# Delta in a Mamba stack: one Softplus pass over four blocks at a time in place of Abs, Relu, Exp and Ln on ScalarE and a sum on GpSimd

## The chip, the cores and the metric

One core of one Trainium2 chip runs the whole program. The metric is the device time of one execution in microseconds (us). The engines are named as the profile names them: PE is TensorE (PEld its weight loads), DVE is VectorE, ACT is ScalarE, POOL is GpSimd, SP is SyncE.

## The reference, cut to what matters

Two Mamba layers over 8192 rows of 512 channels, with layer norms around them, and then a soft mixture of experts. The change is in the Mamba part, in the line that makes `delta`:

```python
xc, z = split(x @ W_in.T)                      # 1024 inner channels each
u = silu(conv4(xc) + b_c)
dt, Bm, Cm = split(u @ W_x.T)                  # 32, 16, 16
delta = softplus(dt @ W_dt.T + b_dt)           # the changed part
h_t = exp(delta_t * A) * h_{t-1} + (delta_t * u_t) * B_t    # 16 states for each channel
y_t = sum_n(h_t * C_t) + u_t * D
x = (y * silu(z)) @ W_out.T
```

Everything is fp32. The weights and inputs are random; softplus(x) was computed before as max(x, 0) + ln(1 + exp(-|x|)).

## The kernel before, in words

The 1024 inner channels are 8 blocks of 128 partitions. The 8192 rows are cut into 16 chunks of T = 512, which lie on the free axis. With two layers there are 32 chunk bodies, one after the other. A body has GROUPS = 32 groups (16 states for each of two halves of four blocks), and each group has four slots, one for each block: 128 slots, numbered s = 0 to 127 below. In slot s

- ACT writes one tile of `decay` = exp(delta * A) into a PSUM ring of four (`decay_of`, line 857; DEC_RING = 4),
- POOL writes, every second slot, one pair of tiles of `bu` = w * B, with w = delta * u (`inputs`, line 1086; p = s // 2 is the pair), into a ring of three pairs,
- DVE runs one scan h = decay * h + bu over 512 steps of time (`scan`, line 1166), and then `add_state` (line 1186), which multiplies a turned state tile with C and adds it to `acc`,
- PE turns the states of the group before (`turn_states`, line 589) into a PSUM ring of two tiles, `turn`. Two of eight such tiles are taken by ACT (`product`, line 873), the others by DVE. ACT also takes the `skip` tiles u * D (lines 597 and 880).

Around these fixed slots a timetable (`ORDER`, `timetable()`) spreads the projections of the next chunk: matmuls on PE into a second PSUM ring of two (`proj`), and on ACT what empties them. Every engine runs its instructions in the written order, and semaphores join them. The tile kinds `delta` (blocks 4 to 7 of this chunk) and `delta_next` (blocks 0 to 3 of the next) are emptied by ACT in `delta_parts`: w = |x| and delta = max(x, 0), one instruction each. When two blocks are there, `softplus_exp` (slot of the tile plus 1) and `softplus_ln` (plus 2) run over the pair (128 x 1024), and POOL adds (`sum_delta`) and multiplies with u (`product`), at the pairs p that `W_AT` lists. ACT takes delta tiles in slots 12, 18, 27, 32 and 84, 86, 93, 94. Exp and ln of the four pairs stand in slots 19 and 20, 33 and 34, 87 and 88, 95 and 96.

Silu of four blocks at once (`silu_u`, `silu_z`) is done in slots 43, 65, 116 and 129 (slot 1 of the next body). It is one ACTIVATE over 128 x 2048 between two table loads: one that the compiler puts ahead of it, and one asked for by `exp_tables()`, after which Exp and Ln can be used again.

Before the first body a prologue computes u, x_proj and delta for half of chunk 0, and only then can the first scan start.

Of the kernel before, what the change touches and what calls it, by code (L numbers as in the profile page):

```python
# [23 lines left out]
HB = NB // 2  # L24
# [33 lines left out]
W_AT = {13: ('sum', 2), 19: ('product', 2), 25: ('sum', 3), 27: ('product', 3), 47: ('sum_next', 0), 51:  # L58
        ('product_next', 0), 56: ('sum_next', 1), 63: ('product_next', 1)}
# [51 lines left out]
def timetable():  # L111
# [5 lines left out]
    for i, (kind, x, earliest) in enumerate(ORDER):  # L117
# [21 lines left out]
        if kind.startswith("delta") and x % 2 == 1:  # L139
            for q, part in enumerate(("exp", "ln")):  # L140
                take[late + 1 + q].append((part + kind[5:], x // 2, i))
# [147 lines left out]
def mamba_stack(nc, ctx, d, rstd, nmr):  # L289
# [75 lines left out]
    exp_set = sem("exp_set")  # L365
    softplus_set = sem("softplus_set")
    delta_set = sem("delta_set")
# [326 lines left out]
    def _(act):  # L694
# [83 lines left out]
        def delta_parts(src, X, b):  # L778

            if b % HB == 0:  # L780
                act.wait_ge(bu_set, X * PAIRS + (b // HB * (PAIRS // 2) - PAIRS // 2 + C_BU))
            act.activation(w[:, b, :], src, ACT.Abs)
            act.activation(delta[:, b, :], src, ACT.Relu).then_inc(proj_done, 1)

        def softplus_exp(X, freed, pair):
            act.wait_ge(proj_done, freed)
            act.activation(w[:, 2 * pair:2 * pair + 2, :], w[:, 2 * pair:2 * pair + 2, :], ACT.Exp, scale=-1.0).then_inc(exp_set, 1)

        def softplus_ln(X, pair):
            act.wait_ge(exp_set, X * HB + (pair + 1))  # L790
            act.activation(w[:, 2 * pair:2 * pair + 2, :], w[:, 2 * pair:2 * pair + 2, :], ACT.Ln, bias=1.0).then_inc(softplus_set, 1)  # L791
# [59 lines left out]
        def decay_of(G, kind, k, b):  # L851
# [3 lines left out]
            if n == 0:  # L855
                act.wait_ge(delta_set, G * HB + (blk // 2 + 1))
# [75 lines left out]
        for pair in range(HB // 2):  # L932
            softplus_exp(X, n + C_PROJ, pair)
            softplus_ln(X, pair)
# [3 lines left out]
        def take_tiles(G, position, kind, now, behind):  # L938


            for what, x, i in TAKE[position]:
# [4 lines left out]
                if not kind.has({"silu_u": "conv", "silu_z": "gate", "exp": "delta", "ln": "delta",  # L946
                                 "exp_next": "delta_next", "ln_next": "delta_next"}.get(what, what)):
                    continue
# [4 lines left out]
                if what not in ("silu_u", "silu_z", "exp", "ln", "exp_next", "ln_next"):  # L953
                    act.wait_ge(proj_full, full)
                if what == "delta":
                    delta_parts(src, G, x)
                if what == "exp":
                    softplus_exp(G, freed + 1, x)
                if what == "ln":
                    softplus_ln(G, x)  # L960
# [16 lines left out]
                if what == "exp_next":  # L977
                    softplus_exp(G + 1, freed + 1, x)
                if what == "ln_next":
                    softplus_ln(G + 1, x)  # L980
# [56 lines left out]
    def _(pool):  # L1037
# [26 lines left out]
        def sum_delta(X, pair):  # L1064

            lo = 2 * pair
            pool.wait_ge(softplus_set, X * HB + (pair + 1))
            pool.tensor_tensor(delta[:, lo:lo + 2, :], delta[:, lo:lo + 2, :], w[:, lo:lo + 2, :], ALU.add).then_inc(delta_set, 1)  # L1068

        def product(X, pair):  # L1070

            lo = 2 * pair
            pool.wait_ge(delta_set, X * HB + (pair + 1))
            pool.wait_ge(u_set, X * 2 + (pair * 2 // HB + 1))
# [37 lines left out]
        for pair in range(HB // 2):  # L1112
            sum_delta(0, pair)
            product(0, pair)

        def delta_w(G, what, pair):
            X = G + what.endswith("_next")
            if what.startswith("sum"):
                sum_delta(X, pair)
            else:  # L1120
                product(X, pair)

        def body(G, kind):
            for p in range(PAIRS):
                what, pair = W_AT.get(p, ("", 0))
                if what and kind.has(what.replace("sum", "delta").replace("product", "delta")):
# [864 lines left out]
```

## Time and profile before

| | |
|---|---|
| median of 3 runs | 7865.79 us (7862.75 to 7871.68) |
| the profiled execution, its own time | 7866.45 us |
| its span in the trace | 7864.7 us |
| first scan of the first body | 124.83 us |
| length of one body, layer 0, layer 1 | about 221.75 us, about 221.0 us |

The span is what the trace covers; the profiled execution took 1.75 us more than that and 0.7 us more than the median of the runs. All times in the timeline rows are us from the start of the span. In a timeline row the first number is the start, the second how long it took (from the start of the first to the end of the last where several are merged, xN), and in brackets stands how long the engine had been idle and what released it.

### The profile page before, as it was taken

The page shows a single profiled execution, that of the slowest core. Times are in us where ns is not written, and L with a number is a line of the kernel's source. Part 1 is how long each engine was busy: PE and PEld are TensorE (multiplying, and loading weights), DVE is VectorE, ACT ScalarE, POOL GpSimd, SP SyncE. Part 2 cuts the span into 40 slices and gives each one's busy share as a digit, 9 for nine tenths or more (in the row PEclk, how much of TensorE's full clock was granted, in tenths as well). Part 3 has the DMA queues.
Part 4 walks back from the last instruction along what each step waited for, and adds up shares of the span by engine and source line. Part 5 has one row for each costly group of instructions (what it writes and reads, how often), then busy time and mean ns, then how long its engine had stood idle before and what let it go on. Part 6 is the DMA issues. An engine that isn't in the chain of part 4 may idle for free. (4 is left out here: it accounts for less than half of the span.)

```text
span 7864.7 us, 100984 instructions
## 1 busy us (share of the span) xinstructions
PE 7131.2 (91%) x31188; PEld 4059.3 (52%) x31188; DVE 7350.3 (93%) x8247; ACT 5888.5 (75%) x11211; POOL 6606.0 (84%) x2870
## 2 busy tenths in 40 slices
PE   7899999999999999998999999999999999977899
PEld 3455555555555555554555555555555555544765
DVE  3999999999999999999999999999999999997745
ACT  6787888887877887777777777777777777764653
POOL 3999999999999999999999999999999999996020
PEclk9999999999999999999999999999999999988798
DMA  2122111112211221121211111111111111111754
GB/s 85 61 65 66 60 65 58 55 61 65 66 65 61 65 65 56 55 66 66 66 56 49 56 52 49 53 54 56 54 56 49 56 54 47 53 49 62 261 208 150
DMA packets 230983, 549.65 MB, mean 70 GB/s; under 512 B 27120, under 2 KB 27376, under 8 KB 210864
## 3 DMA queue, kind: packets, MB, share of 16 engines
q1 hardware_dynamic: 201776, 491.81, 19.5%
q10 hardware_dynamic: 28672, 51.39, 1.7%
q8 instruction: 252, 4.13, 0.2%
q14 instruction: 283, 2.32, 0.1%
HBM read 441.39 MB, written 101.71 MB: 69 GB/s over the span
## 5 line engine op out<-in xcount | busy, mean ns | idle before, releaser
L1086 POOL TENSOR_TENSOR bu<-w,b_rep 128x1024 f32<-128x1024 f32 x2048 | 4810.1, 2368 | 538.9 <-DVE h L1166 529.4
L1166 DVE TENSOR_TENSOR_SCAN h<-decay,h_last,bu 128x512 f32<-128x512 f32 x3840 | 4797.7, 1269 | 13.9 <-ACT decay L857 13.9
L589 PEld LDWEIGHTS turn<-ident_m,h 128*128 128x128 f32 x16384 | 1952.3, 142 | 2702.8 <-DVE acc L1186 1314.3
L857 ACT ACTIVATE decay<-delta,neg_a 128x512 f32<-128x512 f32 x4096 | 2777.0, 690 | 647.6 <-DVE h L1166 611.6
L589 PE MATMUL turn<-ident_m,h 128*128 128x128 f32 x16384 | 2558.4, 280 | 421.0 <-DVE acc L1186 348.0
L1186 DVE SCALAR_TENSOR_TENSOR acc<-turn,c_now,acc 128x512 f32<-128x512 f32 x3072 | 2227.2, 725 | 72.2 <-ACT c_now L885 43.1
L873 ACT ACTIVATE prod<-turn,c_now 128x512 f32<-128x512 f32 x1024 | 701.0, 685 | 504.5 <-PE turn L589 368.6
L1101 POOL TENSOR_TENSOR prod<-prod 128x1024 f32<-128x1024 f32 x448 | 1058.7, 2363 | 10.6 <-ACT prod L873 10.6
L511 PE MATMUL proj<-x_conv,w_in 128*128 128x512 f32 x2048 | 1046.8, 603 | 4.2 <-ACT x_conv L847 0.9
L511 PE MATMUL proj<-conv_in,conv_diag 128*128 128x512 f32 x2048 | 1024.8, 594 | 0.2 <-ACT halo L750 0.2
L511 PE MATMUL proj<-x_gate,w_in 128*128 128x512 f32 x2048 | 1019.8, 595 | 0.0
L511 PE MATMUL proj<-zy,w_out 128*128 128x512 f32 x1024 | 505.6, 596 | 23.0 <-ACT u L758 20.5
L511 PE MATMUL proj<-w_out,zy 128*128 128x512 f32 x1024 | 504.4, 599 | 0.9 <-DVE zy L1195 0.9
L1166 DVE TENSOR_TENSOR_SCAN h<-decay,zeros_m,bu 128x512 f32<-128x512 f32 x256 | 319.3, 1268 | 128.0 <-POOL bu L1086 124.8
L511 PEld LDWEIGHTS proj<-x_conv,w_in 128*128 128x128 f32 x2048 | 328.2, 193 | 123.3 <-issue 91.7
L511 PEld LDWEIGHTS proj<-conv_in,conv_diag 128*128 128x128 f32 x2048 | 325.8, 191 | 106.7 <-issue 103.6
L511 PEld LDWEIGHTS proj<-x_gate,w_in 128*128 128x128 f32 x2048 | 324.1, 191 | 98.0 <-issue 91.8
L1068 POOL TENSOR_TENSOR delta<-delta,w 128x1024 f32<-128x1024 f32 x128 | 302.4, 2362 | 48.0 <-ACT w L791 48.0
L597 PE MATMUL turn<-d_diag,u 128*128 128x128 f32 x2048 | 288.6, 285 | 48.5 <-DVE acc L1186 44.2
L740 ACT ACTIVATE conv_diag<-ident_m,par 128x128 f32<-128x128 f32 x1024 | 326.2, 394 | 0.8 <-ACT x_conv L847 0.5
L1075 POOL TENSOR_TENSOR w<-delta,u 128x1024 f32<-128x1024 f32 x128 | 302.9, 2366 | 0.3
L597 PEld LDWEIGHTS turn<-d_diag,u 128*128 128x128 f32 x2048 | 252.8, 194 | 74.3 <-DVE acc L1186 60.1
(157 smaller groups left out, 5777.7 us busy)
## 6 DMA issues: line engine op xcount, KB each, us to landing
b_rep<-b_rows SPq DMA_DIRECT2D x1024, 256.0 KB, 3.2
x_gate<-xt SPq DMA_DIRECT2D x32, 1024.0 KB, 6.9
xt<-stage ACTq DMA_DIRECT2D x128, 256.0 KB, 2.4
x_conv<-xt SPq DMA_DIRECT2D x31, 1024.0 KB, 6.9
x_gate<-in_x_dram SPq DMA_DIRECT2D x16, 1024.0 KB, 6.6
x_l<-in_x_dram SPq DMA_DIRECT2D x16, 1024.0 KB, 8.7
m_l<-xt SPq DMA_DIRECT2D x16, 1024.0 KB, 4.9
x<-x_l SPq DMA_DIRECT2D x16, 1024.0 KB, 4.9
```

The source lines that it names most:

```text
L511: mm = pe.matmul(out[0:lhs.shape[1], :], lhs, rhs, start=n == 0, stop=n == count - 1)
L589: mm = pe.transpose(out[:, b * P:(b + 1) * P], h[:, (G * GROUPS + k) % H_RING, b, j * P:(j + 1) * P], ident[:])
L597: mm = pe.matmul(out[:, b * P:(b + 1) * P], u[:, hf * HB + b, j * P:(j + 1) * P], d_diag[:, hf * HB + b, :], start=True, stop=True)
L740: act.activation(conv_diag[:, b % 2, k, :], ident[:], ACT.Copy, scale=par[:, STATES + k, b:b + 1])
L857: act.activation(decay[:, (G * SLOTS_BODY + s) % DEC_RING, :], delta[:, blk, :], ACT.Exp, scale=neg_a[:, n, blk:blk + 1]).then_inc(decay_s ...
L873: act.activation(prod[:, V_BUFFER[q], k % 2, :], turn[:, BANK[tile], :], ACT.Copy, scale=c_now[:, j, n:n + 1]).then_inc(v_done, 1)
L1068: pool.tensor_tensor(delta[:, lo:lo + 2, :], delta[:, lo:lo + 2, :], w[:, lo:lo + 2, :], ALU.add).then_inc(delta_set, 1)
L1075: pool.tensor_tensor(w[:, lo:lo + 2, :], delta[:, lo:lo + 2, :], u[:, lo:lo + 2, :], ALU.mult).then_inc(w_set, 2)
L1086: pool.tensor_tensor(bu[:, (G * PAIRS + s // 2) % BU_RING, :, :], w[:, blk:blk + 2, :], b_rep[:, g % B_RING, :].unsqueeze(1).to_broadcast( ...
L1101: pool.tensor_tensor(total, total, prod[:, V_BUFFER[q]], ALU.add).then_inc(vsum_set, 1)
L1166: dve.tensor_tensor_scan(h[:, (G * GROUPS + k) % H_RING, b, :], decay[:, (G * SLOTS_BODY + s) % DEC_RING, :], bu[:, (G * PAIRS + s // 2) % ...
L1186: dve.scalar_tensor_tensor(out, src, scalar, out, ALU.mult, ALU.add).then_inc(x_done, 1)
```

## The change

ACT copies a projected delta tile from PSUM to `delta` with one COPY, instead of writing |x| and max(x, 0). When all four blocks of a half are there, one ACTIVATE Softplus over 128 x 2048 works in place on `delta`, in the slot in which exp of the second pair stood, followed by `exp_tables()`. The passes exp and ln, POOL's sum, and two semaphores go. `decay_of` waits once for each half instead of once for each block. POOL's four products with u are moved by `W_AT`: from p = 19, 27, 51, 63 to 25, 28, 58, 61.

```diff
@@ -55,8 +55,7 @@
 V_SUM_AT = (11, 10, 11, 11, 11, 11, 11, 9, 9, 9, 11, 11, 11, 10, 11, 9)
 JOIN_AT = (41, 72)
 
-W_AT = {13: ('sum', 2), 19: ('product', 2), 25: ('sum', 3), 27: ('product', 3), 47: ('sum_next', 0), 51:
-        ('product_next', 0), 56: ('sum_next', 1), 63: ('product_next', 1)}
+W_AT = {25: ('product', 2), 28: ('product', 3), 58: ('product_next', 0), 61: ('product_next', 1)}
 
 
 NORM_SLOTS = (10, 11, 13, 14, 20, 22, 25, 27, 28, 30, 31, 51, 52, 53, 56)
@@ -136,9 +135,8 @@
         if kind == "conv_half":
             take[late - TAPS_LEAD].append(("taps", x, i))
         take[late].append((kind, x, i))
-        if kind.startswith("delta") and x % 2 == 1:
-            for q, part in enumerate(("exp", "ln")):
-                take[late + 1 + q].append((part + kind[5:], x // 2, i))
+        if kind.startswith("delta") and x % HB == HB - 1:
+            take[late + 1].append(("softplus" + kind[5:], x // HB, i))
         if kind == "conv" and x % HB == HB - 1:
             take[late + SILU_LATER[x // HB]].append(("silu_u", x // HB, i))
         if kind == "gate" and x % HB == HB - 1:
@@ -779,16 +775,12 @@
 
             if b % HB == 0:
                 act.wait_ge(bu_set, X * PAIRS + (b // HB * (PAIRS // 2) - PAIRS // 2 + C_BU))
-            act.activation(w[:, b, :], src, ACT.Abs)
-            act.activation(delta[:, b, :], src, ACT.Relu).then_inc(proj_done, 1)
-
-        def softplus_exp(X, freed, pair):
+            act.copy(delta[:, b, :], src).then_inc(proj_done, 1)
+
+        def softplus(freed, hf):
             act.wait_ge(proj_done, freed)
-            act.activation(w[:, 2 * pair:2 * pair + 2, :], w[:, 2 * pair:2 * pair + 2, :], ACT.Exp, scale=-1.0).then_inc(exp_set, 1)
-
-        def softplus_ln(X, pair):
-            act.wait_ge(exp_set, X * HB + (pair + 1))
-            act.activation(w[:, 2 * pair:2 * pair + 2, :], w[:, 2 * pair:2 * pair + 2, :], ACT.Ln, bias=1.0).then_inc(softplus_set, 1)
+            act.activation(delta[:, hf * HB:hf * HB + HB, :], delta[:, hf * HB:hf * HB + HB, :], ACT.Softplus).then_inc(softplus_set, 2)
+            exp_tables()
 
         def gate(src, b):
 
@@ -852,8 +844,8 @@
             hf, n = divmod(k, STATES)
             blk, s = hf * HB + b, HB * k + b
             act.wait_ge(scanned, G * SLOTS_BODY + (s + 1 - DEC_RING + C_SCAN))
-            if n == 0:
-                act.wait_ge(delta_set, G * HB + (blk // 2 + 1))
+            if n == 0 and b == 0:
+                act.wait_ge(softplus_set, G * HB + (hf * 2 + 2))
             act.activation(decay[:, (G * SLOTS_BODY + s) % DEC_RING, :], delta[:, blk, :], ACT.Exp,
                            scale=neg_a[:, n, blk:blk + 1]).then_inc(decay_set, 1)
 
@@ -1061,17 +1045,13 @@
         bias(0)
         bias(1)
 
-        def sum_delta(X, pair):
+        def product(X, pair):
 
             lo = 2 * pair
-            pool.wait_ge(softplus_set, X * HB + (pair + 1))
-            pool.tensor_tensor(delta[:, lo:lo + 2, :], delta[:, lo:lo + 2, :], w[:, lo:lo + 2, :], ALU.add).then_inc(delta_set, 1)
-
-        def product(X, pair):
-
-            lo = 2 * pair
-            pool.wait_ge(delta_set, X * HB + (pair + 1))
-            pool.wait_ge(u_set, X * 2 + (pair * 2 // HB + 1))
+            half = lo // HB
+            pool.wait_ge(softplus_set, X * HB + (half * 2 + 2))
+            pool.wait_ge(u_set, X * 2 + (half + 1))
+            pool.wait_ge(bu_set, X * PAIRS + (half * (PAIRS // 2) - PAIRS // 2 + C_BU))
             pool.tensor_tensor(w[:, lo:lo + 2, :], delta[:, lo:lo + 2, :], u[:, lo:lo + 2, :], ALU.mult).then_inc(w_set, 2)
 
         def inputs(G, k, pr):
```

What this does to the order of the instructions is shown at three places of a steady body of layer 0. The first is ACT around slot 33, before the change. `acc<-turn` is the copy of a skip tile (slot 33), `w<-w` is exp and then ln over a pair, and `conv_diag` (slot 35) belongs to the convolution.

```order
L782 ACTIVATE w<-proj 128x512
L783 ACTIVATE delta<-proj 128x512
L857 ACTIVATE decay<-delta,neg_a 128x512
L880 COPY acc<-turn 128x512
L787 ACTIVATE w<-w 128x1024
L857 ACTIVATE decay<-delta,neg_a 128x512
L791 ACTIVATE w<-w 128x1024
L857 ACTIVATE decay<-delta,neg_a 128x512
L880 COPY acc<-turn 128x512
L740 ACTIVATE conv_diag<-ident_m,par 128x128 x4
```

And the same place in the changed kernel, with that file's own line numbers:

```order
L778 COPY delta<-proj 128x512
L849 ACTIVATE decay<-delta,neg_a 128x512
L872 COPY acc<-turn 128x512
L782 ACT_TABLE_LOAD
L782 ACTIVATE delta<-delta 128x2048
L701 ACT_TABLE_LOAD
L849 ACTIVATE decay<-delta,neg_a 128x512 x2
L872 COPY acc<-turn 128x512
L736 ACTIVATE conv_diag<-ident_m,par 128x128 x4
```

Between the decay tiles of slots 33 and 34 a load, a pass over four blocks and another load now stand, where one pass over two blocks stood; nothing stands between those of 34 and 35.

The second place is ACT around slot 95, before the change. `prod<-turn` is a state tile that ACT takes for the sum over the states (slots 94 and 95).

```order
L857 ACTIVATE decay<-delta,neg_a 128x512
L873 ACTIVATE prod<-turn,c_now 128x512
L782 ACTIVATE w<-proj 128x512
L783 ACTIVATE delta<-proj 128x512
L857 ACTIVATE decay<-delta,neg_a 128x512
L873 ACTIVATE prod<-turn,c_now 128x512
L787 ACTIVATE w<-w 128x1024
L857 ACTIVATE decay<-delta,neg_a 128x512
L890 COPY h_last<-h 128x4
L791 ACTIVATE w<-w 128x1024
```

And in the changed kernel:

```order
L849 ACTIVATE decay<-delta,neg_a 128x512
L865 ACTIVATE prod<-turn,c_now 128x512
L778 COPY delta<-proj 128x512
L849 ACTIVATE decay<-delta,neg_a 128x512
L865 ACTIVATE prod<-turn,c_now 128x512
L782 ACT_TABLE_LOAD
L782 ACTIVATE delta<-delta 128x2048
L701 ACT_TABLE_LOAD
L849 ACTIVATE decay<-delta,neg_a 128x512
L882 COPY h_last<-h 128x4
```

Here too the whole group now stands between two decay tiles, those of slots 95 and 96.

The third place is POOL from p = 23 to p = 31 of the same body, before the change (`delta<-delta,w` is the sum, `w<-delta,u` the product, `prod<-prod` a sum over states).

```order
L1101 TENSOR_TENSOR prod<-prod 128x1024
L1086 TENSOR_TENSOR bu<-w,b_rep 128x1024
L1068 TENSOR_TENSOR delta<-delta,w 128x1024
L1086 TENSOR_TENSOR bu<-w,b_rep 128x1024 x2
L1075 TENSOR_TENSOR w<-delta,u 128x1024
L1086 TENSOR_TENSOR bu<-w,b_rep 128x1024
L1101 TENSOR_TENSOR prod<-prod 128x1024
L1086 TENSOR_TENSOR bu<-w,b_rep 128x1024 x4
```

And in the changed kernel:

```order
L1081 TENSOR_TENSOR prod<-prod 128x1024
L1066 TENSOR_TENSOR bu<-w,b_rep 128x1024
L1055 TENSOR_TENSOR w<-delta,u 128x1024
L1066 TENSOR_TENSOR bu<-w,b_rep 128x1024 x3
L1081 TENSOR_TENSOR prod<-prod 128x1024
L1055 TENSOR_TENSOR w<-delta,u 128x1024
L1066 TENSOR_TENSOR bu<-w,b_rep 128x1024 x4
```

The product of blocks 4 and 5 stands where the sum of blocks 6 and 7 stood, that of blocks 6 and 7 one pair later than before, and the number of long instructions in the stretch is the same.

## Rows read from the trace of the kernel before

**Rows 1.** The page's first part: busy time, share of the span, instructions.

```profile
PE 7131.2 (91%) x31188; PEld 4059.3 (52%) x31188; DVE 7350.3 (93%) x8247; ACT 5888.5 (75%) x11211; POOL 6606.0 (84%) x2870
```

**Rows 2.** Busy time in one body: stretch, length, PE, PEld, DVE, ACT, POOL.

```profile
3002.40:3224.10 221.70, 205.33 (x917) 115.83 (x916) 218.89 (x233) 178.81 (x345) 205.04 (x90) 0.99 0.18 59
```

**Rows 3.** Waits in the whole span: us in total, times, longest.

```profile
DVE h L1166 <- POOL bu L1086: 124.8, 1, 124.8
...
DVE acc L1186 <- ACT c_now L885: 43.1, 31, 1.4
...
DVE h L1166 <- ACT decay L857: 17.1, 33, 1.9
...
POOL bu L1086 <- DVE h L1166: 529.4, 568, 2.7
```

**Rows 4.** Groups by line: count, busy us, mean ns of one, idle before.

```profile
L1068 POOL TENSOR_TENSOR delta<-delta,w 128x1024 f32<-128x1024 f32 x128 | 302.4, 2362 | 48.0 <-ACT w L791 48.0
...
L796 ACT COPY zy<-proj 128x512 f32<-128x512 f32 x256 | 149.3, 583 | 83.7 <-PE proj L511 83.3
```

**Rows 5.** Timeline of ACT at slot 43, a Silu between its two loads.

```profile
3075.03 1.28 ACT L762 ACT_TABLE_LOAD   x1
3076.33 1.91 ACT L762 ACTIVATE u<-u 128x2048 f32<-128x2048 f32 x1
3078.26 1.28 ACT L705 ACT_TABLE_LOAD   x1
3079.55 1.28 ACT L740 ACTIVATE conv_diag<-ident_m,par 128x128 f32<-128x128 f32 x4
```

**Rows 6.** Timeline of all engines, slots 31 to 35.

```profile
3058.50 1.16 PE L597 MATMUL turn<-d_diag,u 128*128 128x128 f32 x8 [0.34 <-DVE acc L1186]
...
3059.70 0.59 ACT L880 COPY acc<-turn 128x512 f32<-128x512 f32 x1 [0.88 <-PE turn L597]
...
3060.18 1.06 ACT L787 ACTIVATE w<-w 128x1024 f32<-128x1024 f32 x1
...
3061.14 0.68 ACT L857 ACTIVATE decay<-delta,neg_a 128x512 f32<-128x512 f32 x1
...
3063.86 1.27 DVE L1166 TENSOR_TENSOR_SCAN h<-decay,h_last,bu 128x512 f32<-128x512 f32 x1
...
3064.08 0.59 ACT L880 COPY acc<-turn 128x512 f32<-128x512 f32 x1 [0.70 <-PE turn L597]
```

**Rows 7.** Timeline of all engines, slots 37 to 40.

```profile
3070.11 0.68 ACT L873 ACTIVATE prod<-turn,c_now 128x512 f32<-128x512 f32 x1
...
3070.84 1.16 PE L597 MATMUL turn<-d_diag,u 128*128 128x128 f32 x8
...
3074.06 0.60 PE L589 MATMUL turn<-ident_m,h 128*128 128x128 f32 x4
...
3074.74 0.72 DVE L1186 SCALAR_TENSOR_TENSOR acc<-turn,c_now,acc 128x512 f32<-128x512 f32 x1
```

**Rows 8.** Timeline of all engines, slots 93 to 96.

```profile
3162.82 0.60 PE L589 MATMUL turn<-ident_m,h 128*128 128x128 f32 x4
...
3163.45 0.70 ACT L873 ACTIVATE prod<-turn,c_now 128x512 f32<-128x512 f32 x1
...
3164.99 0.69 ACT L857 ACTIVATE decay<-delta,neg_a 128x512 f32<-128x512 f32 x1
...
3168.32 1.27 DVE L1166 TENSOR_TENSOR_SCAN h<-decay,h_last,bu 128x512 f32<-128x512 f32 x1
```

**Rows 9.** Timeline of ACT and POOL around p = 25, slot 48.

```profile
3083.69 2.37 POOL L1068 TENSOR_TENSOR delta<-delta,w 128x1024 f32<-128x1024 f32 x1
...
3085.89 0.69 ACT L758 ACTIVATE u<-proj,par 128x512 f32<-128x512 f32 x1
```

**Rows 10.** Timeline of ACT and POOL at the end of the prologue.

```profile
109.85 0.59 ACT L783 ACTIVATE delta<-proj 128x512 f32<-128x512 f32 x1
...
112.69 2.35 POOL L1068 TENSOR_TENSOR delta<-delta,w 128x1024 f32<-128x1024 f32 x1 [48.03 <-ACT w L791]
...
122.27 4.65 POOL L1086 TENSOR_TENSOR bu<-w,b_rep 128x1024 f32<-128x1024 f32 x2
```

More of the change, by code:

```diff
@@ L364, in mamba_stack @@
     z_set = sem("z_set")
-    exp_set = sem("exp_set")
     softplus_set = sem("softplus_set")
-    delta_set = sem("delta_set")
     w_set = sem("w_set")
@@ L931, in _ @@
             n += 1
-        for pair in range(HB // 2):
-            softplus_exp(X, n + C_PROJ, pair)
-            softplus_ln(X, pair)
+        softplus(n + C_PROJ, 0)
         set_a(0, 0)
@@ L945, in take_tiles @@
                     continue
-                if not kind.has({"silu_u": "conv", "silu_z": "gate", "exp": "delta", "ln": "delta",
-                                 "exp_next": "delta_next", "ln_next": "delta_next"}.get(what, what)):
+                if not kind.has({"silu_u": "conv", "silu_z": "gate", "softplus": "delta",
+                                 "softplus_next": "delta_next"}.get(what, what)):
                     continue
@@ L952, in take_tiles @@
                 src = proj[:, kind.place[i] % RING, :]
-                if what not in ("silu_u", "silu_z", "exp", "ln", "exp_next", "ln_next"):
+                if what not in ("silu_u", "silu_z", "softplus", "softplus_next"):
                     act.wait_ge(proj_full, full)
@@ L956, in take_tiles @@
                     delta_parts(src, G, x)
[L957 to L960, printed above, removed]
+                if what in ("softplus", "softplus_next"):
+                    softplus(freed + 1, x)
                 if what == "conv_half":
@@ L976, in take_tiles @@
                     delta_parts(src, G + 1, x)
[L977 to L980, printed above, removed]
                 if what == "gate":
@@ L1112, in _ @@
         for pair in range(HB // 2):
-            sum_delta(0, pair)
             product(0, pair)
         def delta_w(G, what, pair):
[L1117 to L1121, printed above, removed]
+            product(G + what.endswith("_next"), pair)
         def body(G, kind):
@@ L1125, in body @@
                 what, pair = W_AT.get(p, ("", 0))
-                if what and kind.has(what.replace("sum", "delta").replace("product", "delta")):
+                if what and kind.has(what.replace("product", "delta")):
                     delta_w(G, what, pair)
```

## The prediction

> **What bounds the kernel now.** I began with the page's first part: DVE is busy for 93% of the span, PE for 91%, POOL for 84%, ACT for 75% [rows 1]. Shares say little here, so I took one body by itself. Of its 221.70 us DVE works 218.89 and is idle for 2.8; PE works 205, POOL 205 and ACT 179 [rows 2]. The Mamba part, 32 such bodies, is bound by DVE, whose work the change doesn't touch. Work taken from ACT or POOL can shorten a body by those 2.8 us at most; work put on them can lengthen it wherever DVE comes to wait. In the table of waits, DVE waited for POOL once, before the first scan (124.8 us), never in a body; 31 times for `c_now` (43.1 us); and 33 times for a decay tile (17.1 us), about once a body [rows 3]. POOL waited 568 times for scans (529.4 us), so it runs as far ahead as its ring lets it. So the question is when ACT delivers each decay tile, and I read that in the timeline, having counted the scans of the body that begins at 3002.36 to know the slots.
>
> **What is removed.** In a body of 221 us ACT loses 8 Abs and 8 Relu, whose place 8 copies of 583 ns take [rows 4], and four passes each of exp and ln; POOL loses four sums of 2.36 us [rows 4]. In a body that is worth nothing by itself: DVE waits for neither there, except for the decay tile at slot 44 and for `c_now` at slot 8, and neither place is near the removed passes (slots 19, 20, 33, 34, 87, 88, 95, 96).
>
> **What a Softplus costs on ACT.** The trace has no Softplus. The nearest row is Silu of the same shape between the same two loads: load 1.28 us, pass 1.91 us, load 1.28 us, and from the first load's start at 3075.03 to the next instruction at 3079.55 it is 4.52 us, in which no decay tile is made [rows 5]. From below, the pass can't take less than exp over half the elements, 1.06 us [rows 6], and above I allow a doubled pass, 3.8 us. I take 1.91, the value of the row with the same form. Before, one exp stood in that place and held the next decay tile back by 0.85 us (from the end of the copy, 3059.70 + 0.59 = 3060.29, to 3061.14) [rows 6]. The decay tile behind each Softplus therefore comes 4.52 + 0.01 - 0.85 = 3.68 us later, unless ACT can start the group earlier.
>
> **Slot 33.** ACT can't start earlier here: the copy in front of the group began at 3059.70 after 0.88 us of waiting for PE's skip tile, and PE had itself waited for DVE to free a bank [rows 6]. What the cheaper delta copies save just lengthens this wait. The decay tile of slot 34 was ready at 3061.14 + 0.68 = 3061.82 and its scan began at 3063.86: 2.04 us to spare. DVE will wait 3.68 - 2.04 = 1.65 us. A part of the lateness goes on through the turn ring. ACT takes the skip tile of slot 33 after two decay tiles of 0.61 us each: the first now starts at 3060.29 + 4.53 = 3064.82, so the copy at 3066.04, against 3064.08 before [rows 6], 1.96 us late, 0.3 more than DVE. From there ACT works without a pause to the product at 3070.11, whose end at 3070.79 frees the bank that PE takes at 3070.84 for the last skip tile; and at slot 40 DVE takes its tile at 3074.74, only 0.08 us after PE has made it (3074.06 + 0.60) [rows 7]. So 0.3 less 0.08, about 0.2 us more, reach DVE. Slot 33 costs 1.85 us in each of 32 bodies: 59.2 us. In the bodies where ACT and PE have other margins (the first and last) it can be a little more.
>
> **Slot 95.** The product in front of the group follows PE's tile (3162.82 + 0.60 = 3163.42, taken at 3163.45) [rows 8], so the copies saved before it don't help here either. The decay tile of slot 96 was ready at 3164.99 + 0.69 = 3165.68, its scan began at 3168.32, 2.64 us to spare. DVE waits 3.68 - 2.64 = 1.04 us. Behind it ACT has no ln to do any more and DVE's next tiles are ready on PE, so I count nothing for later. The last body has no `delta_next`: 31 x 1.04 = 32.2 us.
>
> **POOL.** It does two long instructions fewer in each half of a body, and what hides the rest is its ring of three pairs [rows 3]. From p = 23 to 28, where it has least to spare, the number of long instructions stays the same. One edge is new: the copy of u at slot 48 waits for the product of blocks 4 and 5, which overwrites nothing before it is done. That product now stands where the sum started at 3083.69, and so ends at 3086.06; the copy began at 3085.89 [rows 9]. That is 0.2 us on ACT at most, less what ACT is already late by; I take nothing. If that cover were gone, it would be 0.2 x 32 = 6 us.
>
> **Prologue.** The first scan waits for four POOL instructions, from 112.69 to the first `bu` at 122.27 [rows 10], 9.58 us; two of them, 4.63 us, stay. The last delta tile was done at 109.85 + 0.59 = 110.44; with one copy for each tile I put it at 109.55 (between 0 and 2 us earlier). Load and pass take 3.2 us from there, POOL starts at 112.85 and `bu` at 117.5: 4.8 us gained.
>
> **Sum.** 59.2 + 32.2 - 4.8 = 86.6 us. On the profiled execution's own 7866.45 us that is 7953; the median of the runs is 0.7 us less, which I leave out.
>
> **A rule that speaks against this.** The trace has the load at 1.28 us and the pass 0.02 us behind it [rows 5], with no pause in between. The Trainium skill, "ScalarE: Activation LUTs", section "What ACT_TABLE_LOAD costs", gives about 2.66 us for every switch, the load and a drain of 1.38 us; by that the group would take 7.2 us, and the total would be about 8125. The rows don't show that drain between load and pass, so they decide.
>
> **The rivals.**
>
> (a) The group hides: ACT is further ahead than I read, and DVE sees only the prologue, 7862, no change. For it: four Silu groups a body cost DVE only 17.1 us in all [rows 3]. Against it: Silu at slot 43 already makes DVE wait, and the spare times of 2.04 and 2.64 are both below 3.68 [rows 6, 8]. 5%.
>
> (b) On the other side: the relief of ACT reaches the wait for `c_now`. It is worth 43.1 us, with the prologue 48, so 7818. It decides if ACT is late at slot 8 because of its own load over the whole body; but the last of the removed passes stands at slot 96, 40 slots before, and behind it ACT waits for PE and DVE again and again. Even then slots 33 and 95 would have to cost under 32 us together to be faster by the bound. 3%.
>
> (c) Softplus is slower than Silu. With a doubled pass both waits grow by 1.91 us: 63 x 1.91 = 120, so 8074. No row speaks for it: exp, 1.06 us for 1024 elements [rows 6], and Silu, 1.91 us for 2048 [rows 5], lie on one line of 0.83 ns for each. 4%.
>
> (d) A switch to Softplus's set costs more than one to Silu's, as a pause beside each load. With a pause as long as the load itself, 1.28 us [rows 5], it would be 63 x 2.56 = 161, so 8114. The rows 3076.33 and 3079.55 follow their loads by 0.02 and 0.01 us [rows 5]. 2%. This is the case to which the drain of the page would come.
>
> (e) The waits are right, but part comes back: a later DVE gives PE and ACT time, and the decay wait at slot 44 (17.1 us in all, [rows 3]) goes, or the group at 95 starts 0.5 us earlier (15 us). Then about 7925. 13%.
>
> **How the numbers follow.** The forecast (two new waits a body, 1.6 to 2.2 us and 0.9 to 1.3 us, which is 7931 to 7972) has 73%. The range takes in (e) below and, above, 0.4 us more a body for what goes on through the turn ring: 7924 to 7985. A measurement of this kernel can't tell less than 0.2%, 16 us, from no change. Faster 0.03 (b), same 0.06 (a), slower 0.91.
>
> **What would show it.** In the new trace: 64 Softplus rows of 1.91 us, 128 more loads; in DVE's table of waits a decay wait of 1.6 to 1.7 us at slot 34 and one of about 1.0 us at slot 96, some 95 in number and 100 us in total, against 33 and 17.1; bodies of about 224.7 and 223.9 us; the first scan at about 120. The `c_now` wait stays at 43 us. I am wrong if the scan at slot 34 starts without a wait, if Softplus takes another time than Silu, or if the waits for PE's turn tiles grow by more than 0.3 us a body.

## The result and the profile after

The changed kernel takes 7956.87 us in the median of 4 runs (7954.51 to 7967.72), the kernel before beside it 7866.81 us: 1.0117 times as long, 95% interval 1.0099 to 1.0134. The profiled execution took 7956.39 us, its span 7954.6 us, 89.9 us more than before. The page's first part, against [rows 1]:

```profile
PE 7155.0 (90%) x31188; PEld 4052.4 (51%) x31188; DVE 7359.8 (93%) x8247; ACT 5846.8 (74%) x10891; POOL 6321.3 (79%) x2742
```

POOL works 285 us less and ACT 42 us less, and the kernel is 90 us longer. The body of the same number as in [rows 2], in the same columns:

```profile
3042.91:3267.68 224.77, 205.23 (x916) 114.51 (x916) 219.19 (x234) 177.53 (x335) 196.19 (x86) 1.00 0.18 57
```

DVE works as long as before, within 0.3 us, and is idle for 5.6 us in place of 2.8. The waits, against [rows 3]:

```profile
POOL bu L1066 <- DVE h L1141: 918.1, 949, 3.8
...
DVE h L1141 <- POOL bu L1066: 121.5, 1, 121.5
DVE h L1141 <- ACT decay L849: 103.6, 96, 2.4
DVE norm_sq_l L1380 <- PE ssq_l L1487: 73.3, 16, 10.6
...
DVE acc L1161 <- ACT c_now L877: 43.1, 31, 1.4
```

DVE now waits for a decay tile 96 times in place of 33, 103.6 us in place of 17.1; the wait for `c_now` is the same 43.1 us. POOL's freed time went into its own waiting for DVE, 918 us in place of 529. The groups by line, against [rows 4]:

```profile
L782 ACT ACTIVATE delta<-delta 128x2048 f32<-128x2048 f32 x64 | 122.3, 1911 | 0.7
...
L782 ACT ACT_TABLE_LOAD x64 | 82.1, 1283 | 1.2
```

Where the time stands, by the start of each scan in both traces: the first scan is 3.3 us earlier (121.51 against 124.83), the 32 bodies are 100.4 us longer, and what follows the last scan is 7.1 us shorter. The first body is 7.16 us longer, each of the next 30 between 3.00 and 3.10 us, the last 1.34 us. In a body in the middle, the extra time to the next scan is 1.67 us at slot 33, 0.20 at slot 40, 0.09 at slot 43 and 1.09 at slot 95; all other slots are within 0.05 us. The timeline at slots 31 to 35, against [rows 6]:

```profile
3099.01 1.16 PE L593 MATMUL turn<-d_diag,u 128*128 128x128 f32 x8 [0.33 <-DVE acc L1161]
...
3100.20 0.58 ACT L872 COPY acc<-turn 128x512 f32<-128x512 f32 x1 [1.37 <-PE turn L593]
3100.81 1.28 ACT L782 ACT_TABLE_LOAD   x1
3102.10 1.91 ACT L782 ACTIVATE delta<-delta 128x2048 f32<-128x2048 f32 x1
3104.03 1.28 ACT L701 ACT_TABLE_LOAD   x1
3105.32 1.30 ACT L849 ACTIVATE decay<-delta,neg_a 128x512 f32<-128x512 f32 x2
...
3106.05 1.28 DVE L1141 TENSOR_TENSOR_SCAN h<-decay,h_last,bu 128x512 f32<-128x512 f32 x1 [1.60 <-ACT decay L849]
```

ACT had waited 1.37 us for PE's skip tile, so the group could not start sooner; it runs from 3100.81 to 3105.32, and the scan behind it waits. (The row counts 1.60 us of idle time; from scan to scan it is 1.67.) At slot 40, against [rows 7]:

```profile
3114.52 0.58 ACT L872 COPY acc<-turn 128x512 f32<-128x512 f32 x1 [0.55 <-PE turn L593]
...
3116.47 0.60 PE L585 MATMUL turn<-ident_m,h 128*128 128x128 f32 x4
...
3117.11 0.75 DVE L1161 SCALAR_TENSOR_TENSOR acc<-turn,c_now,acc 128x512 f32<-128x512 f32 x1
```

DVE takes this tile 0.04 us after PE has made it: the bank came late. At slots 95 and 96, against [rows 8]:

```profile
3205.26 0.60 PE L585 MATMUL turn<-ident_m,h 128*128 128x128 f32 x4
...
3205.89 0.69 ACT L865 ACTIVATE prod<-turn,c_now 128x512 f32<-128x512 f32 x1 [0.40 <-PE turn L585]
3206.60 1.28 ACT L782 ACT_TABLE_LOAD   x1
...
3211.12 0.69 ACT L849 ACTIVATE decay<-delta,neg_a 128x512 f32<-128x512 f32 x1
...
3211.84 1.28 DVE L1141 TENSOR_TENSOR_SCAN h<-decay,h_last,bu 128x512 f32<-128x512 f32 x1 [1.00 <-ACT decay L849]
```

The end of the prologue, against [rows 10]:

```profile
105.33 0.58 ACT L764 COPY xdbl<-proj 64x512 f32<-64x512 f32 x1 [7.94 <-PE proj L507]
...
110.34 0.59 ACT L778 COPY delta<-proj 128x512 f32<-128x512 f32 x1 [0.27 <-PE proj L560]
...
114.34 4.64 POOL L1055 TENSOR_TENSOR w<-delta,u 128x1024 f32<-128x1024 f32 x2 [47.67 <-ACT delta L782]
118.94 6.96 POOL L1066 TENSOR_TENSOR bu<-w,b_rep 128x1024 f32<-128x1024 f32 x3
```

### The profile page after: what moved, and what is told of

Its sections match the earlier page's. It is cut to its first block and busy times, and to the rows that moved or that the text cites. A ratio compares the mean times of both kernels' runs of the same rounds, so it can differ in the third digit from the quotient of the medians.

```text
span 7954.6 us, 100536 instructions
## 1 busy us (share of the span) xinstructions
PE 7155.0 (90%) x31188; PEld 4052.4 (51%) x31188; DVE 7359.8 (93%) x8247; ACT 5846.8 (74%) x10891; POOL 6321.3 (79%) x2742
## 5 line engine op out<-in xcount | busy, mean ns | idle before, releaser
L1161 DVE SCALAR_TENSOR_TENSOR acc<-turn,c_now,acc 128x512 f32<-128x512 f32 x3072 | 2229.0, 726 | 76.8 <-ACT c_now L877 43.1
L601 PE MATMUL turn<-ident_m,acc 128*128 128x128 f32 x1024 | 166.4, 286 | 126.6 <-DVE acc L1161 114.4
```

Source lines behind the costliest of these rows:

```text
L601: mm = pe.transpose(out[:, j * P:(j + 1) * P], acc[:, hf, j, b * P:(b + 1) * P], ident[:])
L1161: dve.scalar_tensor_tensor(out, src, scalar, out, ALU.mult, ALU.add).then_inc(x_done, 1)
```

## The experiments

The theory: a group on ACT costs DVE its own length, less the pass that it replaced, less the time that the decay tile behind it had to spare; nothing else of the change costs. The rivals: the loads cost by their number; GpSimd's new places cost; the stall is not of ACT's length. In each run the medians of the kernel before were between 7864.7 and 7866.5 us. Lengths of bodies and slots are taken from the starts of the scans and given as the difference from before. In the diffs `...` stands for what is left out.

**No switch, and no long group.** Exp takes Softplus's place, with the table that is there, so that delta has other values.

```diff
-            act.activation(..., ACT.Softplus).then_inc(softplus_set, 2)
-            exp_tables()
+            act.activation(..., ACT.Exp).then_inc(softplus_set, 2)
```

> The changed kernel with Exp in place of Softplus, so that delta is exp(x) and its values differ, and without the two table loads around it: the same pass over 128 x 2048 in the same two slots. My theory is that a group on ACT costs DVE the time by which it makes the next decay tile later, less what that tile had to spare before. The pass alone holds the next tile back by 1.82 us, 0.97 more than exp of a pair did, under the 2.04 and 2.64 us to spare at slots 34 and 96: no new wait, bodies of 221.75 and 221.0 us as before, and a prologue about 6 us shorter: about 7861. If the pass over four blocks at once makes DVE wait and not the loads, it stays above 7900; if each load is paid for in full wherever it stands, it would be 7957 - 164 = 7793.

Measured 7863.3 us, ratio 0.9992 (0.9983 to 1.0002). Waits of DVE:

```profile
DVE h L1140 <- ACT decay L848: 17.0, 33, 1.9
```

The decay waits are those of before. With the two loads gone and all else kept (the copies, the pass over four blocks, POOL's places, one wait for each half), nothing is left of the 90 us. Nor is there a gain beyond the noise from all the work that the change removes.

**The group of the next blocks three slots later.**

```diff
-            take[late + 1].append(("softplus" + kind[5:], x // HB, i))
+            take[late + (4 if kind == "delta_next" else 1)].append(("softplus" + kind[5:], x // HB, i))
```

> The changed kernel with the Softplus of blocks 0 to 3 in slot 98 in place of slot 95. The tile behind it, of slot 99, had 5.3 us to spare before and 3.6 after the change, with the lateness from slot 95 in it; the group makes it 4.5 us later. My theory: the wait of 1.09 us at slot 96 goes and no other comes, 7957 - 35 = 7922, with bodies of 223.7 and 223.0 us. The rival, that a load costs its time wherever it stands, has 7957; one that the turn or projection ring passes the lateness on from slots 98 to 104 has 7930 to 7960.

Measured 7929.08 us, ratio 1.0076 (1.0061 to 1.0091). Waits of DVE:

```profile
DVE h L1141 <- ACT decay L849: 72.1, 65, 2.5
```

The 1.09 us at slot 95 is gone and nothing came in its place: bodies in the middle are 1.97 us longer, 1.68 of it at slot 33, 0.20 at slot 40 and 0.09 at slot 43. So the place sets the cost. The time is 7 us over the expectation. The bodies are as expected; in the profiled runs the stage after them is 8.5 us longer than in the changed kernel (more on it below).

**Both groups moved.** The time tiles 6 and 7 are made earlier, so that the group of blocks 4 to 7 stands in slot 28.

```diff
-         5, 0), ('conv', 1, 0), ('conv_half', 3, 0), ('delta', 6, 0), ('conv', 2, 0), ('delta', 7, 0), ('conv_half',
+         5, 0), ('conv', 1, 0), ('delta', 6, 0), ('conv_half', 3, 0), ('delta', 7, 0), ('conv', 2, 0), ('conv_half',
...
-            take[late + 1].append(("softplus" + kind[5:], x // HB, i))
+            take[late + (4 if kind == "delta_next" else 0)].append(("softplus" + kind[5:], x // HB, i))
```

> As the run before, and the delta projections of blocks 6 and 7 earlier in the order on PE, so that ACT has the last in slot 28 and does the other Softplus in the same slot, with the tile of slot 29 having 5.5 us to spare. My theory: the waits at slots 34, 40 and the growth at 44 go as well (1.97 us in each body), bodies of 221.8 and 221.0 us, and only the prologue's gain is left: 7860, up to 7875 if the moved matmuls press on PE. The rival that loads cost their time anywhere has 7957.

Measured 7880.84 us, ratio 1.0021 (1.0012 to 1.0030). What the changed kernel lost at slots 33, 40, 43 and 95 is gone, but each body in the middle is still 0.5 us longer, nearly all of it at slot 29, and the time is 6 us over the upper end of what I expected. Its timeline there:

```profile
3059.31 1.28 ACT L701 ACT_TABLE_LOAD   x1
...
3060.47 0.60 PE L585 MATMUL turn<-ident_m,h 128*128 128x128 f32 x4
...
3061.85 0.67 ACT L865 ACTIVATE prod<-turn,c_now 128x512 f32<-128x512 f32 x1
...
3062.57 0.65 PE L601 MATMUL turn<-ident_m,acc 128*128 128x128 f32 x4 [0.20 <-ACT prod L865]
...
3063.26 0.69 DVE L1170 TENSOR_TENSOR zy<-turn,zy 128x512 f32<-128x512 f32 x1 [0.28 <-PE turn L601]
```

The decay tiles have the time to spare now, but ACT takes PE's tile (ended 3061.07) only at 3061.85; that holds a bank, PE makes the y tile late, and DVE waits for it. ACT has two dates to keep, and I had reckoned only with one.

**Softplus by pairs.** Four groups a body in place of two, each over 128 x 1024, so twice the loads.

```diff
-        if kind.startswith("delta") and x % HB == HB - 1:
-            take[late + 1].append(("softplus" + kind[5:], x // HB, i))
+        if kind.startswith("delta") and x % 2 == 1:
+            take[late + 1].append(("softplus" + kind[5:], x // 2, i))
...
+            act.activation(delta[:, 2 * pair:2 * pair + 2, :], delta[:, 2 * pair:2 * pair + 2, :], ACT.Softplus).then_inc(softplus_set, 1)
```

> The changed kernel with Softplus over pairs of blocks (128 x 1024), each between two loads, in the four slots in which exp stood (19, 33, 87, 95): twice the groups and loads. A group takes 1.28 + 1.06 + 1.28 + 0.04 = 3.67 us and makes the next tile 2.83 us later than exp did. With 2.98, 2.04, 2.37 to 2.64 and 2.64 us to spare, less what the cheaper copies give, my theory has waits of 0, 0.8 (0.2 more through the turn ring), 0 to 0.4 and 0.2 us: 1.2 to 1.6 us in a body, 7900 to 7918, so faster than the changed kernel in spite of twice the loads. If the cost is that of the loads, it doubles: about 8045.

Measured 7927.84 us, ratio 1.0077 (1.0062 to 1.0093). Waits of DVE:

```profile
DVE h L1142 <- ACT decay L849: 52.8, 99, 1.9
```

Twice the loads and 29 us less than the change. Slot 33 costs 0.82 us in place of 1.67, slot 95 0.23 in place of 1.09: both less by what the group is shorter, a pass over 1024 elements less. New are 0.23 us at slot 87 and, in layer 0, 0.41 at slot 22, where DVE waits for PE's y tile as in the run before this one. That makes 1.60 us a body in layer 1, as forecast, but 2.02 in layer 0 and 7.8 in the first body, and the time was some 10 us above the range that I gave.

**GpSimd's places alone, in the kernel before.**

```diff
-W_AT = {13: ('sum', 2), 19: ('product', 2), 25: ('sum', 3), 27: ('product', 3), 47: ('sum_next', 0), 51:
-        ('product_next', 0), 56: ('sum_next', 1), 63: ('product_next', 1)}
+W_AT = {13: ('sum', 2), 25: ('product', 2), 19: ('sum', 3), 28: ('product', 3), 47: ('sum_next', 0), 58:
+        ('product_next', 0), 51: ('sum_next', 1), 61: ('product_next', 1)}
```

> The kernel before, with GpSimd's products of w and sums of delta put where the changed kernel has its products (pairs 25, 28, 58 and 61 for the products); nothing else. My theory, that the time comes from ScalarE's group alone and GpSimd's places are worth nothing: 7866, within 10 of it, and each body within 0.2 us of before. The rival, that the later products hold up the copy of u or the product of the next pair: some 0.2 us a body, 7872; if the places were the cause of most of the change's loss, 7900 or more.

Measured 7871.87 us, ratio 1.0007 (0.9997 to 1.0016). Bodies of layer 0 are some 0.2 us longer (at slot 62; the first two are 2.2 and 1.9 longer), those of layer 1 are as before. The 5 us by which the medians differ are within what this measurement can't tell from no change. So the places are no cause of the 90 us; in the changed kernel slot 62 isn't longer at all. But the rival's 0.2 us a body is there in layer 0, and the rows tell how it comes about. In the sixth body ACT's product in slot 61 waits 1.15 us for POOL's sum over states, in place of 0.69 before, and so frees its bank later; in slot 62 DVE waits 0.72 us for PE's tile, in place of 0.49.

**The group at slot 26.** From here on the versions go after what was left of the two moved groups. Here both time tiles are made ahead of the half product 3 and taken in slots 23 and 24.

```diff
-         5, 0), ('conv', 1, 0), ('conv_half', 3, 0), ('delta', 6, 0), ('conv', 2, 0), ('delta', 7, 0), ('conv_half',
+         5, 0), ('conv', 1, 0), ('delta', 6, 0), ('delta', 7, 0), ('conv_half', 3, 0), ('conv', 2, 0), ('conv_half',
...
-            take[late + 1].append(("softplus" + kind[5:], x // HB, i))
+            take[late + (4 if kind == "delta_next" else 2)].append(("softplus" + kind[5:], x // HB, i))
```

> The changed kernel with both groups where ScalarE has the time for them: the time tiles 6 and 7 are made before the half product 3 (taken in slots 23 and 24), Softplus of blocks 4 to 7 stands in slot 26, that of the next blocks in slot 98. My theory, that only the places of the two groups cost: the body loses the 0.5 us at slot 29 that the version with the group in slot 28 had, since ScalarE starts the group two slots earlier and is level again when its product of slot 30 is due; bodies within 0.2 us of before, and the whole 7860 to 7872. The rival, that a group of 4.47 us fits nowhere at that stage, since about 4.6 to 5 us is the most by which ScalarE is ahead: again 0.3 to 0.8 us a body, 7876 to 7892.

Measured 7868.52 us, ratio 1.0003 (0.9994 to 1.0012): not to be told from before. But only the bodies of layer 1 are as before (within 0.01 us, but for three), with the last two of layer 0; the first is 4.3 us longer and the 13 behind it 0.43, all at slot 29. So theory and rival each hold in one layer.

**SiLU one slot later too**, added to the version in slot 26, to use the decay wait that is there in every body of the kernel before, and **SiLU one slot later in the kernel before**:

```diff
-SILU_LATER = (1, 2, 4, 3)
+SILU_LATER = (2, 2, 4, 3)
```

> The version before this one, with SiLU of u's first half in slot 44 in place of 43, where the kernel before already waits 0.56 us for a decay in every body. By my theory of spare time the decay of slot 44 is then in time and those of 45 and 46 come 0.05 and 0.25 us late: 0.3 us a body won, 10 us in all, 7850 to 7862, faster than the kernel before. The rival, that ScalarE's two products of slots 46 and 47 then come late and the turn ring holds PE: no gain or a loss, 7865 to 7885.

> The kernel before with only SiLU of u's first half in slot 44 in place of 43, beside the last one, to tell what this move gives without the change. By my theory the same 0.3 us a body, 7852 to 7860. The rival, the turn ring: 7866 or more.

Measured 7880.42 us, ratio 1.0017 (1.0008 to 1.0026), and 7862.18 us, ratio 0.9995 (0.9986 to 1.0004). In both, slot 43 is 0.56 us shorter, and slots 44, 45 and 46 are 0.09, 0.21 and 0.17 us longer: 0.09 us a body won where I had expected 0.3. The wait was moved, not removed; the one at slot 46 I hadn't foreseen. Both times are over the ranges that I gave, the first by 18 us and inside the rival's.

In the first of them, nine bodies are a further 1 to 1.7 us longer, six at slot 24 and three at slots 62 to 64, and DVE waits there for a tile of PE. The trace shows TensorE slower just there, and at neither place in any other body but the last. In the body that begins at 4565.92 its granted clock, as a share of the full 2.4 GHz, is 0.92 in slot 22, 0.50 (the lower of its two levels, 1.2 GHz) in slot 23 and 0.80 in slot 24; in the body before that, with slot 24 as usual, it is 1.00 in all of them. In both bodies PE had worked for just 0.73 of the 2.41 us of slot 22, so what made the clock fall in one and not in the other stays open. Single bodies of the other versions that are 1 us longer at slot 24, and the second body of the run with GpSimd's places, at slots 63 and 64, show slow matmuls of the same kind.

**The group at slot 25**, to the version in slot 26.

```diff
-            take[late + (4 if kind == "delta_next" else 2)].append(("softplus" + kind[5:], x // HB, i))
+            take[late + (4 if kind == "delta_next" else 1)].append(("softplus" + kind[5:], x // HB, i))
```

> As the version with the group in slot 26, but in slot 25, and the loads and Softplus of the next blocks in slot 98 again. The profile of the version in slot 26 has its layer 1 bodies at 0.00 us over before and its layer 0 bodies at 0.43, all in slot 29, where ScalarE takes the product of slot 28 1.15 us after PE ended it. In slot 25 the group is one slot more ahead of that product. My theory, that only the place costs: layer 0 bodies within 0.1 us of before too, 14 bodies of 0.43 less, 6 us: 7858 to 7868, no difference from before that this can tell. The rival, that the decay of slot 26 is late, since ScalarE is only 4.83 us ahead there in layer 0: again 0.3 to 0.5 us a body, and as before 7864 to 7874.

Measured 7876.02 us, ratio 1.0015 (1.0006 to 1.0024), though its profiled run took 7867.11. Bodies of layer 1 are as before, those of layer 0 still 0.46 us longer at slot 29. The rival's 0.3 to 0.5 us a body came out, but not its mechanism, since the decay of slot 26 is in time. The timeline of a body of layer 0:

```profile
3056.66 0.71 ACT L817 ACTIVATE stage<-x_gate,neg_mean 128x512 f32<-128x512 f32 x1
...
3058.06 0.72 ACT L817 ACTIVATE stage<-x_gate,neg_mean 128x512 f32<-128x512 f32 x1
...
3058.93 0.66 PE L585 MATMUL turn<-ident_m,h 128*128 128x128 f32 x4 [0.32 <-DVE acc L1161]
...
3060.77 0.67 ACT L865 ACTIVATE prod<-turn,c_now 128x512 f32<-128x512 f32 x1
...
3062.19 0.69 DVE L1170 TENSOR_TENSOR zy<-turn,zy 128x512 f32<-128x512 f32 x1 [0.36 <-PE turn L601]
```

ACT takes the tile 1.2 us after PE ended it at 3059.59. In front of it stand two squares of a normalisation, which only the first 14 bodies do.

**The normalisation's steps later.** To the version before this:

```diff
-NORM_SLOTS = (10, 11, 13, 14, 20, 22, 25, 27, 28, 30, 31, 51, 52, 53, 56)
+NORM_SLOTS = (10, 11, 13, 14, 20, 22, 31, 33, 34, 36, 37, 51, 52, 53, 56)
```

> The version with the groups in slots 25 and 98, and of the normalisation of a later block, which only layer 0 bodies do, three squares and the two small steps after them taken out of slots 25, 27, 28, 30 and 31 and put into 31, 33, 34, 36 and 37. The trace of the version before this one shows two of these squares, some 0.9 us each, between the end of ScalarE's group and the product of slot 28, taken 1.19 us after PE ended it. My theory, that ScalarE's lateness at slot 28 is all that is left: the layer 0 bodies, at 0.46 us over before, come to within 0.1 us of it, 14 of them, 6 us: 5 to 7 us under the version before. The rival, that the squares are late in their new places and hold the products of slots 31 to 38: again 0.3 to 1 us a body, no better than the version before.

Measured 7868.03 us, ratio 1.0001 (0.9992 to 1.0010). ACT now waits for PE there:

```profile
3056.05 0.69 ACT L865 ACTIVATE prod<-turn,c_now 128x512 f32<-128x512 f32 x1 [0.93 <-PE turn L585]
```

The 0.46 us at slot 29 is gone, so it was ACT's lateness at this tile. But 0.20 us at slot 40 and 0.09 at slot 43 are back, as in the changed kernel: the squares, now at 31 to 34, make ACT late for the skip tiles, and a body of layer 0 is 0.28 us longer. So part of the lateness was only moved: I had expected these bodies within 0.1 us of before, and the rival had 0.3 or more. The time is 8 us under the version in slot 25, but the bodies together are only 3 us shorter. Its last two bodies, without the squares, are 1.1 us longer at slot 24, with the slow matmuls told of above. Layer 1 stays as before.

**A second load of the same table, and one of another.** The first adds `exp_tables()` a second time, the second:

```diff
             act.activation(..., ACT.Softplus).then_inc(softplus_set, 2)
+            act.preload_act_table_set("silu_and_others")
             exp_tables()
```

> The changed kernel with the table load that follows Softplus issued twice, so each group of 4.47 us becomes 5.75. My theory, that a group costs its own length less the time that ScalarE is ahead, and the two places of the changed kernel are already past that: each of the 1.28 us is paid in full, 2.56 us a body, 79 us over 31 bodies: 8036, and 8030 to 8042. If the second load of a set that is there costs nothing, 7957. The rival, that the stalls of the changed kernel are of another cause than ScalarE's length (a wait for POOL or for PE's turn ring): a small part of it, under 8000. If each load also stops ScalarE's queue for longer than its row, over 8050.

> The changed kernel with one table load more in each group, of SiLU's table, between Softplus and the load of Exp's, so that a group is 5.75 us and not 4.47. (In the run with the second load of the same table the trace showed no more loads than before: 193 and 64, so nothing was tried there.) My theory, that both places are past the time by which ScalarE is ahead: the 1.28 us is paid in full twice a body, 2.56 us, 79 us over 31 bodies, 8036, and 8030 to 8045 with growth at the turn ring. The rival, that the stalls of the changed kernel are not of ScalarE's length: under 8000. If each load also stops ScalarE's queue for longer than its row, over 8050.

The first had no load more than the changed kernel:

```profile
L701 ACT ACT_TABLE_LOAD x193 | 247.6, 1283 | 7.5 <-POOL ident_m L1037 4.1
```

So the 8036 us that I expected of a longer group wasn't tested by it, and it is a second measurement of the same instructions: 7966.05 us, ratio 1.0129 (1.0115 to 1.0144), bodies together 101.0 us longer against the 100.4 of the changed kernel. The second measured 8075.2 us, ratio 1.0265 (1.0249 to 1.0281). Its timeline at slots 33 to 38, and its decay waits:

```profile
3150.15 1.91 ACT L782 ACTIVATE delta<-delta 128x2048 f32<-128x2048 f32 x1
3152.08 1.28 ACT L783 ACT_TABLE_LOAD   x1
3153.37 1.28 ACT L701 ACT_TABLE_LOAD   x1
3154.66 1.30 ACT L850 ACTIVATE decay<-delta,neg_a 128x512 f32<-128x512 f32 x2
...
3155.39 1.28 DVE L1142 TENSOR_TENSOR_SCAN h<-decay,h_last,bu 128x512 f32<-128x512 f32 x1 [2.89 <-ACT decay L850]
3155.91 0.57 ACT L873 COPY acc<-turn 128x512 f32<-128x512 f32 x1
...
3156.53 1.07 PE L585 MATMUL turn<-ident_m,h 128*128 128x128 f32 x4 [2.46 <-ACT acc L873]
...
3157.39 2.06 PE L593 MATMUL turn<-d_diag,u 128*128 128x128 f32 x8
...
3159.49 0.59 ACT L873 COPY acc<-turn 128x512 f32<-128x512 f32 x1 [0.54 <-PE turn L593]
...
3163.10 0.60 PE L585 MATMUL turn<-ident_m,h 128*128 128x128 f32 x4
...
3163.74 0.75 DVE L1162 SCALAR_TENSOR_TENSOR acc<-turn,c_now,acc 128x512 f32<-128x512 f32 x1 [0.99 <-PE turn L585]
```

```profile
DVE h L1142 <- ACT decay L850: 181.1, 96, 3.8
```

Slot 33 is 2.96 us longer than before in place of 1.67, slot 95 2.37 in place of 1.09: both by 1.29 us more, the length of the row of a load, as expected. The time is still 39 us over the expectation. Of the 115.8 us by which its bodies together are longer than those of the changed kernel, 82.0 stand at these two slots, 33.8 at slot 38 (and 9.9 less at slots 40 and 43) and 8.2 at slot 102. Slot 38 is 0.85 to 1.56 us longer in 26 of the first 31 bodies, 1.12 in the body of [rows 2]; in the other five, all of layer 1, it is as before, and slots 40 and 43 have the 0.20 and 0.09 us of the changed kernel.

The rows tell how slot 38 comes to it. The skip tile of slot 33, which PE ended at 3152.60, is taken at 3155.91, and PE has waited 2.46 us for that. Then it runs at half its pace: the eight matmuls of the next skip tile take 2.06 us, where those of the one before took 1.06. So that tile is only there at 3159.45, and the tile for slot 38 at 3163.70, after DVE has waited 0.99 us for it. TensorE's granted clock is 1.00 up to 3153.89, 0.59 from 3156.49 to 3157.29, 0.50 to 3159.19, 0.67 to 3160.49 and 1.00 again behind that. In the body that begins at 4006.73, one of the five, PE waits the same 2.46 us, the clock stays at 1.00 through these slots, and slot 38 is as before. All of the 26 bodies have such slow matmuls at slots 35 to 37, and none of the five has. In the changed kernel PE waits 1.17 us at this place and the clock stays at 1.00. So the growth that I had put at nothing is TensorE's slower clock behind the pause, and not lateness that grows by itself in the turn ring; what lets the clock stay up in the five bodies is open. That the time is over 8050 is not the rival of a longer stop of ACT's queue: the two slots behind the loads show 1.29 us more, which is the row's length, and no more.

## Why the prediction was right, step by step

**The bound.** DVE bound the bodies before and does after; taking 285 us of work from POOL and 42 us from ACT gave DVE nothing. The run with Exp shows this with all of the removals in place: 7863.3 us.

**The group on ACT.** 4.52 us was taken from SiLU's rows; it is 4.51 (3100.81 to 3105.32), with the pass at 1911 ns. Rivals (c) and (d) fall with that row: no doubled pass, no pause beside the loads. Of the Trainium skill, "ScalarE: Activation LUTs", section "What ACT_TABLE_LOAD costs": its drain of 1.38 us for each switch is not seen here either, since one switch more made DVE 1.29 us later.

**Slot 33.** 1.65 us was forecast and 1.67 measured; 0.2 through the turn ring was forecast, and 0.20 at slot 40 and 0.09 at slot 43 measured. The second of these was missed. (3.68 less 2.04 is 1.64; that changes nothing.)

**Slot 95.** 1.04 forecast, 1.09 measured, and nothing behind it, as said. Moving that group alone took exactly this away.

**POOL.** Nothing, as said. The edge that I had priced at 0.2 us at most, the copy of u behind the product of blocks 4 and 5 [rows 9]:

```profile
3126.06 2.40 POOL L1055 TENSOR_TENSOR w<-delta,u 128x1024 f32<-128x1024 f32 x1
...
3128.55 0.69 ACT L754 ACTIVATE u<-proj,par 128x512 f32<-128x512 f32 x1
```

The copy starts 0.09 us behind the product's end, and no scan behind it is late.

**Prologue.** 4.8 us was forecast and 3.3 came. The chain behind x_proj is as reckoned: from its copy at 105.33 to the first `bu` it is 13.61 us. In the kernel before, that copy stood at 103.72:

```profile
103.72 0.58 ACT L768 COPY xdbl<-proj 64x512 f32<-64x512 f32 x1 [8.32 <-PE proj L511]
```

There it was 18.55 us to `bu` at 122.27 [rows 10], 4.94 more. The missing 1.6 us was lost ahead of it, where the change does nothing. Why is open; over the versions the first scan stands anywhere between 119.7 and 126.0 us.

**The sum.** 86.6 us forecast, 89.9 in the spans. The parts are further off than the sum. The first body is 7.16 us longer, where the sum had 2.89 and the text "a little more": slot 33 costs 2.15 there and slot 95 2.51, and slots 8, 70, 99 and 102 another 2.2 together. TensorE's granted clock is 0.89 in that body and 0.70 in its slots 64 to 97 (0.89 and 0.67 before), where it is 1.00 in the body of the same number as in [rows 2], so the spare times read there don't hold in it. How much of the 7.16 us comes from that isn't shown.

The 30 bodies behind it came to 91.9 in place of 86.7, the last to 1.34 in place of 1.85. So the bodies cost 9.0 us more than forecast and the prologue gave 1.5 less. Against that stands a stage of which the prediction spoke nowhere: after the last scan, the time to the end is 7.1 us shorter than before.

That the sum came within 3.3 us is in part luck: without this stage the kernel would be some 97 us longer, still inside the range. The forecast's narrower band was also added up wrong: 32 waits of 1.6 us and 31 of 0.9, less the prologue's 4.8, give 7941 as its lower end and not 7931. The measured time is inside either way.

The shorter stage is not the change's. It lies in the logits of the mixture behind the Mamba part, where DVE waits 80.6 us for `ssq_l` before and 73.3 after. The run with the second `exp_tables()` has the instructions of the changed kernel, and:

```profile
DVE norm_sq_l L1381 <- PE ssq_l L1488: 79.7, 16, 10.3
```

The kernel before with only GpSimd's places changed has the short one:

```profile
DVE norm_sq_l L1405 <- PE ssq_l L1512: 73.8, 16, 10.9
```

Both delta schemes show both lengths. What sets it stays open. Over all versions its length differs by up to 8.5 us, and in two versions the profiled run, with the short stage, is also the fastest (7865.72 under a median of 7871.87, 7867.11 under 7876.02). So the changed kernel's own loss may be nearer to the 97 us of prologue and bodies than to 90, and expectations of a time are blurred by that much.

**Rival (e)**, that part comes back, did not happen: slot 44's wait of before is there as it was, beside the new ones (96 waits, 33 + 32 + 31). **Rivals (a) and (b)** fall with the 63 new waits and with `c_now` at 43.1 us.

**What the loss hung on.** The places of the two groups. With both groups moved, to slots 26 and 98, the same change measures 7868.52 us, no different from before; its bodies of layer 1 are those of before, those of layer 0 still 0.43 us longer. No version beat the kernel before by more than the noise, as is to be expected where no wait of DVE in a body had been caused by the removed work.

## What to carry to other kernels

When a stage is bound by one engine and another feeds it through a short ring, price a longer group on the feeding engine slot by slot: its length, less what it replaces, less the time that the next tile had to spare in the timeline. Busy shares and the count of instructions say nothing of it; here one engine had 285 us less work and another 42, and the kernel became 1.2% slower. Look for each thing that the feeding engine owes (here the decay tiles and the turn banks) and put the group where it is ahead of all of them; and don't expect anything from relieving engines that the bound doesn't wait for. Where a lateness comes out larger than the ring explains, look at the granted clock of TensorE in that stretch.

## What the runs showed of the hardware

Softplus over 128 x 2048 took 1911 ns, the same as SiLU, with a table load of 1283 ns on each side and 0.01 to 0.02 us between the rows; one load more of another table in each group cost DVE 1.29 us at each of the two slots behind the groups, where ACT was late already. A second request for a table, right behind one for the same table, left no row in the trace (193 loads from that line, as without it) and cost nothing that the bodies show (101.0 us against 100.4). And a longer pause of TensorE can cost more than its own length: with the group 1.28 us longer, PE waited 2.46 us for a bank, its granted clock fell to 0.50 and eight matmuls took 2.06 us in place of 1.06, which reached DVE as 1.12 us at slot 38. The same pause left the clock at 1.00 in five of 31 bodies, and one of 1.17 us in the changed kernel left it there too.
